# A transformer block with routed experts on one core: the next step's normalised rows behind the attention's rows, the Gram product one unit later, and an intermediate matrix in PSUM

## The reference

```
x = x + 0.5 * ffn(layernorm(x))
x = x + attention(layernorm(x))
x = x + 0.5 * ffn(layernorm(x))

ffn(h):   2 shared experts and 16 routed ones; a router takes 4 of the 16 for each token
          y = sum over experts of weight * (silu(h @ gate) * (h @ up)) @ down
attention(h): q, k, v = h @ Wqkv.T + b;  a = q k^T in 32 heads of 4 channels, no softmax
          ctx = a v;  ctx = a normalisation of each channel group over the sequence (gn_w, gn_b)
          out = ctx @ out_w.T + out_b
```

## Time and profile before

| | |
|---|---|
| median of three runs | 649.8 us |
| the profiled execution's own time | 649.93 us |
| its span, first to last instruction | 648.2 us |
| PE busy | 636.3 us, 98% |
| PE weight loads busy | 526.5 us, 81% |
| DVE busy | 522.5 us, 81% |
| POOL busy | 463.9 us, 72% |
| ACT busy | 394.4 us, 61% |
| granted TensorE clock, mean | 1.000 |

### The profile page before, as it was taken

The page is one execution under the profiler, slowest core; times in us unless marked ns, Lnnn a source line. Parts: engine busy times, 40 slices in busy tenths (PEclk is TensorE's granted clock), DMA queues, the critical chain, the costliest instruction groups (busy, mean ns, idle before and its releaser), DMA issues.

```text
span 648.2 us, 9973 instructions
## 1 busy us (share of the span) xinstructions
PE 636.3 (98%) x2927; PEld 526.5 (81%) x2927; DVE 522.5 (81%) x1546; ACT 394.4 (61%) x783; POOL 463.9 (72%) x401
## 2 busy tenths in 40 slices
PE   8999999999999999999999999999999999999997
PEld 7888888888878888788887888878888888888886
DVE  6898888787968879678797798877988878777674
ACT  4876656566575656755667556575565656655554
POOL 6997767767766677676767667676777776777664
PEclk9999999999999999999999999999999999999999
DMA  8727362634438244383353742726627263451710
GB/s 235 261 78 261 67 260 55 213 94 125 178 87 257 73 118 178 82 214 130 93 202 81 187 145 52 272 71 147 208 52 276 50 207 121 117 203 26 277 33 32
DMA packets 128342, 94.26 MB, mean 145 GB/s; under 512 B 84112, under 2 KB 110624, under 8 KB 128288
## 3 DMA queue, kind: packets, MB, share of 16 engines
q1 hardware_dynamic: 128288, 93.63, 47.1%
HBM read 81.55 MB, written 12.06 MB: 144 GB/s over the span
## 4 chain that ended last, share of the span: by engine, by line
PE 83%; DVE 7%; ACT 4%; POOL 3%; issue 2%; DVEq 0%; ACTq 0%; POOLq 0%
PE gateP L547 9%; PE gateP L551 9%; PE upP L551 9%; PE gateP L548 9%; PE upP L547 9%; PE upP L548 9%; PE yP L551 9%; PE yP L547 8%; PE yP L548 8%; ACT XA L863 2%; DVE A L1385 1%; PE attP L617 1%; POOL A_lo L426 1%; ACT XN L830 1%; PE yP L674 1%
## 5 line engine op out<-in xcount | busy, mean ns | idle before, releaser
L426 POOL TENSOR_TENSOR A_lo<-A,A_hi 128x512 fp32r<-128x512 f32 x287 | 369.7, 1296 | 131.9 <-ACT A_hi L907 131.6
L933 ACT ACTIVATE gateP<-gateP 128x512 f32<-128x512 f32 x252 | 146.5, 581 | 196.8 <-PE gateP L551 196.2
L1324 DVE TENSOR_TENSOR T<-gateP,CB 128x512 f32<-128x512 f32 x252 | 173.6, 689 | 96.0 <-ACT gateP L933 92.3
L907 ACT CAST A_hi<-A 128x512 fp32r<-128x512 f32 x287 | 175.9, 613 | 12.5 <-DVE A L1385 11.6
L1385 DVE TENSOR_TENSOR A<-upP,T 128x512 f32<-128x512 f32 x254 | 173.8, 684 | 2.9
L547 PE MATMUL gateP<-XT_hi,W_hi 128*128 128x512 f32 x288 | 116.3, 404 | 0.0
L547 PE MATMUL yP<-A_hi,W_hi 128*128 128x512 f32 x288 | 112.4, 390 | 0.0
L551 PE MATMUL gateP<-XT_lo,W_hi 128*128 128x512 f32 x288 | 112.3, 390 | 0.0
L551 PE MATMUL yP<-A_lo,W_hi 128*128 128x512 f32 x288 | 112.3, 390 | 0.0
L548 PE MATMUL gateP<-XT_hi,W_lo 128*128 128x512 f32 x288 | 112.2, 389 | 0.0
L548 PE MATMUL yP<-A_hi,W_lo 128*128 128x512 f32 x288 | 112.1, 389 | 0.0
(11 more groups left out here) (233 smaller groups left out, 628.4 us busy)
## 6 DMA issues: line engine op xcount, KB each, us to landing
CB<-combT SPq DMA_DIRECT2D x126, 512.0 KB, 7.2
y_rows<-YB SPq DMA_DIRECT2D x60, 64.0 KB, 1.9
YP<-y_rows SPq DMA_DIRECT2D x15, 256.0 KB, 2.8
x_rows<-XN SPq DMA_DIRECT2D x13, 256.0 KB, 2.3
XB<-x_rows SPq DMA_DIRECT2D x52, 64.0 KB, 2.3
xa_rows<-XA SPq DMA_DIRECT2D x4, 512.0 KB, 5.0
W_in<-xa_rows SPq DMA_DIRECT2D x16, 128.0 KB, 2.9
out_dram<-X SPq DMA_DIRECT2D x7, 256.0 KB, 9.1
```

Source lines behind the costliest of these rows:

```text
L426: pool.tensor_tensor(A_lo[:, slot, :], A[:, slot, :], A_hi[:, slot, :].bitcast(F32), ALU.subtract).then_inc(low_done, 1)
L907: act.copy(A_hi[:, v % SLOTS, :], A[:, v % SLOTS, :]).then_inc(high_done, 1)
L933: act.activation(dst, gateP[u % 2][:, :], ACT.Silu).then_inc(silu_done, 1)
L1324: dve.tensor_tensor(T[:, u % TS, :], silu, weights, ALU.mult).then_inc(gate_weighted, 1)
```

## The change

In the first step of a pair with attention the four XN instructions of ACT stand in unit 10 and no longer in unit 9; in the other steps nothing is moved. The attention's stages that follow XA go one unit later as far as GS, s_row, Gn, Gc and nmu: the Gram product from unit 10 to 11, GS from 11 to 12, s_row and Gn, and Gc and nmu, from 12 to 13. PE's products of unit 14 and all that follows stay where they are. Mf is written to columns 128 to 255 of attP, a PSUM bank, and read from there for Mm; the tile Mf in SBUF is left to brow.

```diff
 def attention_stage(u, b):            # PE
-    if u == 10:
+    if u == 11:
         pe.wait_ge(xa_ready, b + 1)   # Gram product
 def attention_stage(u, b):            # ACT
-                if u == 11:
+                if u == 12:
                     act.wait_ge(att_pe, ATT_PE * b + 1)
                     act.copy(GS[:, :], attP[:, 0:P + 1]).then_inc(att_act, 1)
-                if u == 12:
+                if u == 13:
                     act.wait_ge(att_act, ATT_ACT * b + 1)
 def pair(p, first, attention, last):  # ACT
-                    if w in ((15, 16) if early else (9,)) and not last:
+                    if w in ((15, 16) if early else (10 if attention and s == 0 else 9,)) and not last:
                         for part in (w - 15,) if early else (0, 1):
                             normalise(t0 + s + 2, 2 * ((p + 1) % BATCH) + s, part)
 def attention_stage(u, b):            # DVE
-                if u == 12:
+                if u == 13:
                     dve.wait_ge(att_act, ATT_ACT * b + 1)
                 if u == 18:
                     dve.wait_ge(att_pe, ATT_PE * b + 3)
-                    dve.scalar_tensor_tensor(Mf[:, :], rv[:, :], bk[:, :], attP[:, 0:P],
+                    dve.scalar_tensor_tensor(attP[:, P:2 * P], rv[:, :], bk[:, :], attP[:, 0:P],
                                              ALU.mult, ALU.add).then_inc(att_seq, 1)
                     dve.wait_ge(att_seq, v + 11)
-                    dve.tensor_tensor(Mm[:, :], Mf[:, :], blk1[:, :], ALU.mult).then_inc(att_seq, 1)
+                    dve.tensor_tensor(Mm[:, :], attP[:, P:2 * P], blk1[:, :], ALU.mult).then_inc(att_seq, 1)
```

## The result

The changed kernel takes 641.82 us, the median of four runs (641.74 to 641.91), against 649.84 us for the kernel before (649.76 to 650.26). The ratio is 0.9875 with a 95% interval of 0.986 to 0.9891: 8.0 us faster, where 7.8 were forecast. The profiled execution took 641.74 us with a span of 640.0.

What follows compares the result with a forecast made beforehand. PE, busy 98% of the span, was taken to bound the kernel; removing its Gram and Mm stalls, 4 x (1.58 + 0.375) = 7.8 us, took 649.8 to 642.0 us, range 641.2 to 643.8.

Steps and rivals of the forecast that it cites:

- Gram wait: PE's Gram product waits for ACT's last XA; 1.58 us lost per attention, all of it to go.
- the shown idle time (1.33): PE's own idle time at the Gram product, 1.33 us, used only for the lower bound of the gain.
- Mm wait: L632 on PE waits for DVE's Mm; 0.375 us per attention goes whole, Mm falling from 1.25 to 0.28 us.
- the unseen price of the write: Writing Mf to PSUM: price bounded by 0 and 0.28 us, taken as 0.
- Cover behind the move: ACT's silu and T of unit 11 come later; PE's gate product of unit 13 has 2.0 us of cover.
- SP's chain: x_rows is issued later, shifting XB and SP's following work, at worst 2.2 us later against PE; nothing stalls.
- The first case of the two: On SP, xa_rows and x_rows together still need 5.9 us; XB is issued at 273.1, cost nothing.
- The length of the pair: Time of the xa_rows and x_rows transfers together on SP, 5.9 us before, assumed still needed after.
- The cover of 2.95: Slack of the T of unit 20 for CB's first load, landing 7.2 us after issue by the median: 2.95 us.
- slower than before: Rival: late x_rows delays CB and T of unit 20; needs 5.2 us of delay; 651 or over; chance 0.015.
- The sum: Four attentions: 4 x (1.58 + 0.375) = 7.8 us, giving 642.0 us.
- that alone would be enough for PE: XN's move brings `xa_ready` 1.56 us earlier, at 267.17, before PE is free at 267.29.

Runs made afterwards that it cites:

- 72 probes: Changed kernel plus one unread DVE product of ident times blk1, all in SBUF, per even unit of the pairs with attention; 646.23 us, ratio 0.9945.
- unit 13's run: Changed kernel with XN in unit 13 in place of unit 10 in the attention's first step; 642.27 us, ratio 0.9885.

## Why the prediction was right

- **Gram wait, 1.58 per attention: right.** 1.56 by the later product alone, 1.52 by XN's move alone. The reading of the stall from starts and not from the shown idle time (1.33) is what made the size right.
- **Mm wait, 0.375: right.** 0.35 alone, 0.41 on top of the rest. Mm came out at 0.291 and not 0.281, and L1271, which now writes PSUM, at 0.339 and not 0.330 us by its median: the unseen price of the write is 0.01 us, inside the bounds of 0 to 0.28. With two inputs in SBUF 45 of 72 probes were held to the end of POOL's instruction; with one input in PSUM Mm starts 0.2 us into an A_lo and takes 0.29. The rule of the Trainium skill, "SBUF — State Buffer", "Who interferes with whom", is that two such instructions exclude each other for their whole length. The trace agrees, in both directions.
- **Cover behind the move: right.** 2.0 us forecast, 2.2 read after, 2.1 by overloading it. GS, s_row and Gn stalled nobody: Gn ends 1.63 us before L623 in all four attentions, where 1.6 was forecast.
- **SP's chain: right that it costs nothing, the figures in it were loose.** XB was issued at 270.85, 3.3 us after x_rows and not 5.4. Measured against L623 of PE, it was issued 278.87 - 274.63 = 4.2 us ahead before, and 275.04 - 270.85 = 4.2 after; over the four attentions 4.2 to 4.4 before and 4.1 to 5.1 after. So the chain fell back against the stream by 0.2 us at most, though x_rows itself did. The first case of the two held in its mechanism: in every attention, before and after, x_rows landed 0.70 to 0.74 us behind xa_rows, however late it was issued, and where nothing stood before it (unit 13) it landed in 2.3. The Trainium skill, "DMA: Bandwidth & Descriptors", "Queues, rings and completion order", says that a DMA engine takes the descriptors of one ring in order. The trace agrees. The length of the pair, which the prediction held fixed at 5.9, was 5.0 to 6.0 after. The cover of 2.95 was taken with the median landing of a queue of eight loads; with the landing of the first, the one that matters, it is 5.9 in the attention before, and 6.0 by the run with 16 loads more. Nor did the prediction count the 2.05 us from T to PE. It put the first cost at 2.95 us of delay and slower than before at 5.2; by the runs T waits from about 6 and PE from about 8. But once there it costs more than its stalls, by the clock.
- **The sum.** 7.8 forecast, 7.9 by the pairs, 8.0 by the times; the spans differ by 8.2, of which 0.3 lie in the start of the execution.
- **What the prediction did not see:** that the two halves of the move are alternatives. It named the first ("that alone would be enough for PE") and left the consequence out: the later Gram product would have done without XN's move, which brings nothing that can be measured.

## What to carry to other kernels

When an engine waits at a point for data of another, compare when the data are there with when the engine could be there: making the data earlier and making the use later are alternatives, and the second costs nothing when there is other work to fill in. In this kernel a DVE product of two SBUF operands that starts inside a POOL instruction lasts until that instruction is over; with POOL busy 72% of the time, one operand in PSUM was the way out, and its price was a hundredth of a microsecond. An engine's slack is no reason to call such a product free: 72 of them on an engine that is 81% busy cost 4.4 us. Take the landing of a DMA from its own place in its queue, not from the median of the group.

## What the runs showed of the hardware

- A DVE product of 128 by 128 with two inputs in SBUF and a POOL product exclude each other. The DVE one ends 0.145 to 0.151 us after the POOL instruction in which it starts (45 of 45) and takes 0.25 to 0.29 otherwise. A POOL instruction that begins beside it ends 1.14 to 1.17 us after it (40 of 40) and takes up to 1.48 us where 1.30 is usual. The second half was read from the same run and not tested by a run of its own.
- With one input in PSUM the same product took 0.291 us inside an A_lo, and writing that input to PSUM took 0.339 us where SBUF took 0.330.
- A stall of PE of 3.4 us and more was followed in each of four cases by a stretch at the lower clock (granted clock 0.50, starts 0.43 us apart) of 2.7 to 6.1 us, which added 9 us to 15 us of stalls. Stalls of 1.5 us in the kernel before and of 0.9 in the run with eight more ACT instructions had no such tail: the granted clock behind them is 1.00, their first spacing is 0.31 to 0.34 us and the next 0.23 to 0.24.
- Eight CB loads of 512 KB issued behind one another landed 4.1, 4.9, 5.9, 6.4, 7.4, 9.2, 9.9 and 10.8 us after their own issues (unit 13's run, second attention).
